# Attention and a ternary feed-forward layer on one core: value products in two column halves, and a new order of work

## The reference, cut to what matters

```python
y = x * rsqrt(mean(x * x) + 1e-6) * rms_w
q, k, v = split(y @ w_in.T)          # 32 x 64, 8 x 64, 8 x 64
q, k = rope(q), rope(k)
attn = softmax(where(causal, q @ k.T / 8, -inf))
o = attn @ v                         # 4 heads of a group share v
x = layernorm(x + x + o @ w_out.T)
xq = ternary(x, 0.33, 0.5)
x = layernorm(x + x + xq @ (ternary(weight, 0.2, 0.6) + rram_variation).T)
```

## Time and profile before

| | |
|---|---|
| median of 3 runs | 1411.08 us (1410.71 to 1412.4) |
| the profiled execution's own time | 1412.32 us |
| its span, first to last instruction | 1410.5 us |
| PE busy | 1290.8 us (92%), 7328 products |
| DVE busy | 1182.6 us (84%) |
| ACT busy | 1107.7 us (79%) |
| POOL busy | 849.9 us (60%) |
| mean granted TensorE clock | 0.983 |
| the eight bodies begin at | 47.1, 230.9, 389.9, 548.8, 708.1, 867.9, 1026.6, 1186.2 us |
| last turned unit | 1375.6 us |

### The profile page before, as it was taken

How to read it: one execution, slowest core, us unless ns; L and a number is a source line. 1 busy time by engine, 2 the same in 40 slices (tenths; PEclk the granted TensorE clock), 3 DMA queues, 4 the chain that set the end, 5 groups by cost and what they waited for, 6 DMA issues and landing times. The chain is left out here.

```text
span 1410.5 us, 25319 instructions
## 1 busy us (share of the span) xinstructions
PE 1290.8 (92%) x7328; PEld 757.5 (54%) x7328; DVE 1182.6 (84%) x3062; ACT 1107.7 (79%) x2327; POOL 849.9 (60%) x904
## 2 busy tenths in 40 slices
PE   4689998999989999999989999999989999898886
PEld 2355555555545555555645555555645555454554
DVE  4688887989898898988898898989898898888976
ACT  5768778788888888788888788788888888686654
POOL 1356666386746765376646766386646766785565
PEclk9799999999999999999999999999999999999999
DMA  6101111111101201111101211021101211110002
GB/s 201 27 20 44 59 31 32 29 55 46 39 20 47 59 27 31 29 56 46 38 21 46 59 29 31 24 61 45 37 22 42 59 33 50 50 44 25 19 32 86
DMA packets 45163, 61.82 MB, mean 44 GB/s; under 512 B 10464, under 2 KB 27104, under 8 KB 45024
## 3 DMA queue, kind: packets, MB, share of 16 engines
q1 hardware_dynamic: 45024, 60.20, 14.4%
HBM read 34.74 MB, written 4.46 MB: 28 GB/s over the span
## 5 line engine op out<-in xcount | busy, mean ns | idle before, releaser
L799 ACT ACTIVATE prob_hi<-t 128x512 f16<-128x512 f32 x576 | 340.2, 591 | 142.9 <-PE t L1225 137.8
L1104 DVE SCALAR_TENSOR_TENSOR prob_lo<-t,prob_hi 128x512 f16<-128x512 f32 x576 | 394.5, 686 | 58.8 <-ACT prob_hi L799 52.9
L831 ACT ACTIVATE prob<-prob,neg_max 128x896 f32<-128x896 f32 (+7 forms) x512 | 391.9, 767 | 8.9 <-DVE neg_max L1011 7.0
L1169 PE MATMUL s<-k_t,q_t 128*128 128x512 f16 (+3 forms) x1536 | 350.2, 330 | 32.3 <-DVE neg_max L1011 11.9
L1225 PE MATMUL t<-ident,prob 128*128 128x128 f32 x2304 | 351.5, 276 | 6.8 <-ACT prob L831 6.7
L1011 DVE CUSTOM_DVE_ANT_0 prob<-s,mask,neg_kappa 128x512 f32<-128x512 f32 (+3 forms) x512 | 320.0, 644 | 42.2 <-PE s L1169 24.8
L1225 PEld LDWEIGHTS t<-ident,prob 128*128 128x128 f32 x2304 | 290.5, 142 | 106.5 <-ACT prob L831 13.7
L1140 PE MATMUL ot<-prob_lo,v_sb 128*128 128x512 f16 x576 | 221.5, 385 | 29.8 <-DVE prob_lo L1104 28.9
L1138 PE MATMUL ot<-prob_hi,v_sb 128*128 128x512 f16 x576 | 220.4, 383 | 1.3 <-DVE o_raw L1085 1.0
L772 POOL TENSOR_TENSOR o_lo<-o_raw,o_hi 128x256 f16<-128x256 f32 x128 | 86.1, 672 | 196.3 <-ACT o_hi L907 194.7
L1169 PEld LDWEIGHTS s<-k_t,q_t 128*128 128x128 f16 x1536 | 137.5, 99 | 122.7 <-DVE neg_max L1011 37.2
(11 more groups left out here) (105 smaller groups left out, 1815.9 us busy)
## 6 DMA issues: line engine op xcount, KB each, us to landing
swapped<-flat SPq DMA_DIRECT2D x320, 64.0 KB, 2.0
spread<-recip_rows SPq DMA_DIRECT2D x128, 128.0 KB
recip_rows<-turned SPq DMA_DIRECT2D x512, 0.5 KB
raw<-L_attn_w_in SPq DMA_DIRECT2D x8, 768.0 KB, 4.2
raw<-L_attn_w_out SPq DMA_DIRECT2D x8, 512.0 KB, 3.6
out<-acc SPq DMA_DIRECT2D x16, 256.0 KB, 2.0
acc<-L_attn_x SPq DMA_DIRECT2D x3, 1024.0 KB, 10.4
acc<-L_attn_x SPq DMA_DIRECT2D x4, 256.0 KB, 3.2
```

The source lines that it names most:

```text
L799: act.activation(prob_hi[:, u % 2, :], t_ps[u % 2][:, :], ACT.Copy, scale=P_SCALE).then_inc(prob_hi_done, 1)
L831: act.activation(row, row, ACT.Exp, bias=neg_max[:, kk % 4, h:h + 1], scale=-1.0, accum_out=total[:, kk % 4, h:h + 1]).then_inc(ex_done, 1)
L1104: dve.scalar_tensor_tensor(out=prob_lo[:, u % 2, :], in0=t_ps[u % 2][:, :], scalar=P_SCALE, in1=prob_hi[:, u % 2, :], op0=ALU.mult, op1=AL ...
L1169: mm = pe.matmul(s_ps[:, off:off + cols], q_t[:, h, s * P:(s + 1) * P], k_t[:, part, keys:keys + cols], start=(part == 0), stop=(part == 1))
```

## The change

There are four edits.

**The products of step 4.** A unit now takes six products of 256 columns with 64-wide stationary blocks, in place of two of 512 columns with a 128-wide block. The 512 probability columns are cut into two halves of two heads each. The first half goes to rows 0 to 63 of the bank and the second to rows 64 to 127, so the two products of a pair use the left and the right 64 columns of the array. There are three pairs: low value part with `prob_hi`, high part with `prob_hi`, high part with `prob_lo`. The fourth combination, low with low, which the 128-wide block made on the way, is no longer formed. The order of the four heads within `t_ps` changes to fit.

**Batches.** `prob_hi` and `prob_lo` get eight slots, and the products of several units are done one behind the other: `BATCHES` cuts the 36 units of a sequence into 11 batches of one to five.

**The output chain.** Rows 0 to 63 and 64 to 127 now hold finished sums of different heads. So `oe` goes away: ScalarE's `o_low` and VectorE's two additions, and `on` moves from GpSimd to VectorE, which multiplies the bank by `spread` in one instruction. VectorE then waits for `spread`.

**The tables.** All places are new, in all four tables.

```diff
+P_RING = 8
+BATCHES = (1, 2, 3, 4, 5, 3, 3, 4, 3, 4, 4)
+def batch_ending(u):
+    ends = list(itertools.accumulate(BATCHES))
+    return BATCHES[ends.index(u % UNITS + 1)] if u % UNITS + 1 in ends else 0
...
 MIDDLE = dict(
-    SCORES=(((0, 2, 2, 2), (3, 4, 6, 8), 24, 79), ((6, 7, 10, 24), (23, 29, 32, 36), 43, 114),
...
+    SCORES=(((0, 0, 0, 3), (6, 1, 0, 4), 8, 55), ((3, 9, 14, 21), (21, 34, 28, 36), 91, 94),
...
-        for kind, lag in zip(("oe", "on", "oh", "op"), at_pass["OUTPUT"][b * NT + s + 1]):
+        for kind, lag in zip(("on", "oh", "op"), at_pass["OUTPUT"][b * NT + s + 1]):
...
-        prob_hi = sb("prob_hi", [P, 2, BANK], F16)
-        prob_lo = sb("prob_lo", [P, 2, BANK], F16)
-        o_low = sb("o_low", [DH, BANK])
+        prob_hi = sb("prob_hi", [P, P_RING, BANK], F16)
+        prob_lo = sb("prob_lo", [P, P_RING, BANK], F16)
@@ GpSimd @@
-                        elif e[0] == "on":
-                            wait(pool, o_raw_done, g, 2 * NT, kk + 1)
-                            wait(pool, spread_in[kk % 2], g, 16 * NT, 16 * (kk // 2 + 1))
-                            pool.tensor_tensor(o_raw[:, :, :], o_raw[:, :, :], spread[:, kk % 2, :, :], ALU.mult
-                                               ).then_inc(o_t_done, 1)
@@ ScalarE @@
-                        wait(act, pv_done, g, BODY, u - 1)
-                        act.activation(prob_hi[:, u % 2, :], t_ps[u % 2][:, :], ACT.Copy, scale=P_SCALE
+                        wait(act, pv_done, g, BODY, u - P_RING + 1)
+                        act.activation(prob_hi[:, u % P_RING, :], t_ps[u % 2][:, :], ACT.Copy, scale=P_SCALE
...
-                        elif e[0] == "oe":
-                            wait(act, pv_done, g, BODY, b * UNITS + first_unit(s + 1))
-                            wait(act, o_raw_done, g, 2 * NT, k)
-                            act.activation(o_low[:, :], ot_ps[k % 2][DH:P, :], ACT.Copy, scale=1.0 / P_SCALE
-                                           ).then_inc(o_low_done, 1)
@@ VectorE @@
-                        elif e[0] == "oe":
-                            wait(dve, o_low_done, g, 2 * NT, kk + 1)
-                            wait(dve, o_lo_done, g, 2 * NT, kk)
-                            top = ot_ps[kk % 2][0:DH, :].rearrange("p (c a q) -> p a c q", c=2, a=2)
-                            low = o_low[:, :].rearrange("p (c a q) -> p a c q", c=2, a=2)
-                            for a in range(2):
-                                mm = dve.scalar_tensor_tensor(out=o_raw[a * DH:(a + 1) * DH, :, :], in0=top[:, a],
-                                                              scalar=1.0 / P_SCALE, in1=low[:, a], op0=ALU.mult, op1=ALU.add)
-                            mm.then_inc(o_raw_done, 1)
+                        elif e[0] == "on":
+                            wait(dve, pv_done, g, BODY, b * UNITS + first_unit(s + 1))
+                            wait(dve, spread_in[kk % 2], g, 16 * NT, 16 * (kk // 2 + 1))
+                            wait(dve, o_lo_done, g, 2 * NT, kk)
+                            dve.scalar_tensor_tensor(out=o_raw[:, :, :],
+                                                     in0=ot_ps[kk % 2][:, 0:2 * P].rearrange("p (c q) -> p c q", c=2),
+                                                     scalar=1.0 / P_SCALE, in1=spread[:, kk % 2, :, :],
+                                                     op0=ALU.mult, op1=ALU.mult).then_inc(o_t_done, 1)
@@ TensorE @@
-                    values_t = v_sb[:, b % 2, j, :]
-                    pe.matmul(ot_ps[k % 2][:, :], values_t, prob_hi[:, u % 2, :], start=(j == 0), stop=False)
-                    wait(pe, prob_lo_done, g, BODY, u + 1)
-                    pe.matmul(ot_ps[k % 2][:, :], values_t, prob_lo[:, u % 2, :], start=False, stop=(j == s)
-                              ).then_inc(pv_done, 1)
+                    v_hi, v_lo = v_sb[:, b % 2, j, 0:DH], v_sb[:, b % 2, j, DH:P]
+                    def product(values_t, part, first, last):
+                        for a in range(2):
+                            mm = pe.matmul(ot_ps[k % 2][a * DH:(a + 1) * DH, 0:2 * P], values_t,
+                                           part[:, u % P_RING, a * 2 * P:(a + 1) * 2 * P], start=first, stop=last)
+                        return mm
+                    product(v_lo, prob_hi, j == 0, False)
+                    product(v_hi, prob_hi, False, False)
+                    wait(pe, prob_lo_done, g, BODY, u + 1)
+                    product(v_hi, prob_lo, False, j == s).then_inc(pv_done, 1)
...
                         for h in range(HG):
-                            mm = pe.transpose(t_ps[u % 2][:, h * P:(h + 1) * P],
+                            at = (h % 2 * 2 + h // 2) * P
+                            mm = pe.transpose(t_ps[u % 2][:, at:at + P],
...
                     if 0 < u <= plan.units or u == 0 and plan not in (first, opening):
-                        values(u - 1)
+                        for n in range(batch_ending(u - 1)):
+                            values(u - batch_ending(u - 1) + n)
```

More of the change, by code:

```diff
@@ L1 @@
+import itertools
 from contextlib import ExitStack
@@ L648, in pool_idle @@
                     wait(pool, o_scale_done, g, 1, 1)
-                elif kind == "on":
-                    wait(pool, o_t_done, g, 2 * NT, what[0] * NT + what[1] + 1)
                 elif kind == "oh":
```

78 lines of the change are left out of this document (36 added, 42 removed), and 106 rows, old and new, of tables (FIRST, LAYER, PROJECT, SCORES).

## The result

| | before | changed |
|---|---|---|
| median | 1411.74 us (1410.71 to 1414.71, 4 runs) | 1395.36 us (1394.25 to 1399.51, 4 runs) |
| ratio | | 0.9886 [0.9861, 0.9911] |
| profiled span | 1410.5 us | 1393.6 us |
| mean granted TensorE clock | 0.983 | 0.984 |

The change made the kernel 16 us faster. The forecast was 28 us, 1383. The size is off by 12 us, and the time did not come from where the forecast had it.

What follows compares the result with a forecast made beforehand. TensorE sets the pace, with VectorE's lateness adding some 7%. Per body -7.2 (products) + 5.9 (borders) - 2.0 (idle) = -3.3 us, -26.4 over eight bodies, and 1.75 less at the end: 1383 us, range 1330 to 1442.

Steps and rivals of the forecast that it cites:

- The products: TensorE's value products: pairs run side by side, a unit takes 0.33 us for 0.43, saving 7.2 us per body.
- no overlap: Rival: the halves' products run one behind the other, 0.66 us per unit, +118 us, about 1528; chance 0.10.
- The borders: TensorE entering and leaving the 22 half-width batches per body: 0.27 us per batch, 5.9 us per body added.
- the full stop of 0.58: Rival of dear borders at each batch: at 0.58 us, +3.6 per body, 1438 us in all; chance 0.17.
- The output chain: Each pass's end: one VectorE instruction of 425 ns for two of 415, 6.5 us per body saved; ScalarE, GpSimd lighter.
- The wait for `spread`: VectorE's new wait before the output multiplication: costed at nothing, shortest lead 2.5 us, typical 8, longest DMA trip 5.76.
- VectorE stands at `spread`: Rival: the wait passes to TensorE, +5.6 us per body at full price, 1444; at half, 1421; chance 0.08.
- The idle time: TensorE's gaps from VectorE's lateness: 2.0 us per body regained through eight slots and fewer waits for `prob_lo`.
- The tail: Behind the last pass, once: the chain to the end is shorter by 1.75 us.

Runs made afterwards that it cites:

- the run with the constant: Changed kernel, but VectorE multiplies the finished bank by a constant tile in place of `spread`, with no wait for it: 1370.37 us, 0.9705.
- the runs with later places: Changed kernel with `on` later in the tables where VectorE stood at `spread`: 1367.55 us; then middle-body pass 10 moved again, from 30 to 39: 1363.20 us.
- the first move of `on`: Changed kernel with `on` of passes 5, 9 and 10 later by 11 to 18 eighths, likewise three opening and three last-body places: 1367.55 us, 0.9681.
- the best version: Kernel with the later `on`, and `on` of pass 10 in the middle bodies later by another 9 eighths of a unit: 1363.20 us, 0.966.

## Why the prediction was right, and where it was not

It was right in direction, and 1395 lies in the range of 1330 to 1442. By steps:

- **The products.** Right: side by side, 0.33 us for a unit, -7.2 us per body. The rival "no overlap" is excluded. "TensorE: Matmul & The Clock Gate" of the Trainium skill (Part 3) has tiles of one array starting about 4 ns apart, and packing by columns close to packing by rows; the trace agrees, with 3 to 4 ns.
- **The borders.** Mis-sized, high: 0.19 us per batch for 0.27, so 4.2 us per body for 5.9. "TensorEngine Tiling (Array Packing)" of the Trainium skill (Key Properties) states a drain at such a change. The trace has a gap there, 0.09 us in and 0.10 out, much less than the full stop of 0.58, and the first product starts 0.07 us before the record of the last turning ends. Whether the gap is a drain no run shows.
- **The output chain.** Right: 417 ns for 425, and VectorE, ScalarE and GpSimd within 2 us of the forecast over the whole run.
- **The wait for `spread`: the step that failed.** The prediction said of it "I cost it at nothing", with the lead of `rs` over `on` (8 us typical, 2.5 shortest) against one DMA of 5.76 us. That is the wrong lead and the wrong length. The trip begins when `turned` is written, at `rc`, and SyncE's list is part of it: it took 8.9 us in pass 5, 13.2 in pass 9 and 15.7 in pass 10. In the new middle table `rc` stands 24, 36 and 34 eighths of a unit ahead of `on` there, 6.6, 9.9 and 9.4 us. These three passes stood. The lead of `rs` doesn't tell them apart: in pass 9 it is 28 eighths, 7.7 us, and VectorE stood 3.1, while the shortest, 9 eighths in pass 13, made no stand (`rc` is 50 ahead of `on` there). The typical lead was long enough; 13 of 16 passes don't stand, but for one time 0.4 us. The wait cost 25 us by the run with the constant, and 28 and 32 by the runs with later places. The rival "VectorE stands at `spread`" was the case, with a chance of 0.08: its condition, over 3 us per body, was met with 7.5, and its price at half, 2.8 us of idle time per body, is near the 3.2 below.
- **The idle time.** Forecast at 2.0 us per body less. TensorE's work is 147.4 - 7.2 + 4.2 = 144.4 us, so its idle time is 159.3 - 144.4 = 14.9, where it was 11.7: 3.2 more (2.8 in the bodies with a clock of 1.00). Work (-3.0) and idle time (+3.2) cancel, and the middle body stays at 159 us. With the wait gone, idle time is 154.8 - 144.4 = 10.4, which is 1.3 less than before; the 2.0 would then have been near.
- **The tail.** Mis-sized: 1.75 us taken for the end of the chain, but 17 us came in the last body, 5.6 of them behind the last turned unit. I had read the new `LAYER` table as one edit among all places and gave it no term. The run with its old places is 24 us slower, though not all of that need be what the new ones are worth.

So that the total came near the forecast is luck: two errors of opposite sign. With the constant the change brings 41 us, 13 more than the 28 forecast, and the wait takes 25 of them back.

## What to carry to other kernels

Where an instruction moves to a fuller engine, its waits move with it. Price a wait by the whole trip from the last write of its source to the moment it can be read, in us, with what stands ahead of its DMAs in the issuing engine's list, and hold the lead over that same stretch against it, pass by pass. A typical value hides the few passes that stand. Putting the one operand in question as a constant shows in a single run what such a wait costs; then move the waiting instruction later, and not to another engine whose list has due times. And count each table or list that an edit touches as a term of its own. Compare bodies at the same granted clock before a difference of 1 or 2 us is explained.

## What the runs showed of the hardware beyond the forecast

- Products in the left and the right 64 columns run beside each other even when the program has three of one ahead of three of the other: starts in another order than the program's, in pairs about 10 ns apart, 0.33 us for a unit in both.
- Going from 128-wide four-byte turnings into 64-wide products costs 0.09 us, and back 0.10; 112 more such visits made the kernel 13 us slower. The 64-wide weight loads hide behind the products: a pair follows each 0.11 us with no gap.
- Reciprocals of 4 x 128 numbers, sent to main memory and back to all partitions, can be read 8.0 to 8.6 us after the first row DMA is issued (passes 9 and 10), of which the last leg is 4.5. Counted from the write of `turned` it was 8.9 to 15.7 us in the three passes that stood, by what stood ahead in SyncE's list.
- In the changed kernel's middle bodies the granted clock fell to half three times, to the level of 1.2 GHz for 3.4 us each, and each time TensorE had just stood 1.3 to 2.1 us for `acc`. A body with such a fall took 1 us more than one without (160.0 against 158.9). The three falls with the constant and the one after the first move of `on` came within or right behind stands of 2.1 to 2.4 us. In the best version there is no fall, though one stand of 2.1 us is left, so not every stand brings one.
